# Cross-attention and feed-forward in one kernel: the preparation of the weights in another order

## The reference

```
h = layernorm(x)
q = h @ Wq;  k = context @ Wk;  v = context @ Wv          # 8 heads of 128
x = x + softmax(q k^T / sqrt(128)) v @ Wo + bo
h = layernorm(x)
logits = h @ Wr;  prob = trunc(softmax of the top two logits)
x = x + sq_relu(h @ Ws1) @ Ws2 + sum over experts of prob * (sq_relu(h @ W1) @ W2)
```

## Time and profile before

| | |
|---|---|
| median of 3 runs | 119.76 us (119.48 to 120.51) |
| the profiled execution | 119.6 us, of which the trace spans 117.8 us |
| PE busy | 110.2 us, 94% of the span |
| DVE, ACT, POOL busy | 89.2, 85.0, 62.4 us |
| granted clock of PE, mean | 0.997 of full speed |

### The profile page before, as it was taken

The page is one execution under the profiler, slowest core; times in us unless marked ns, Lnnn a source line. Parts: engine busy times, 40 slices in busy tenths (PEclk is TensorE's granted clock), DMA queues, the critical chain, the costliest instruction groups (busy, mean ns, idle before and its releaser), DMA issues.

```text
span 117.8 us, 3097 instructions
## 1 busy us (share of the span) xinstructions
PE 110.2 (94%) x848; PEld 105.3 (89%) x848; DVE 89.2 (76%) x341; ACT 85.0 (72%) x346; POOL 62.4 (53%) x101
## 2 busy tenths in 40 slices
PE   6999989999899989999999999999999999989950
PEld 6988879998798889999999999999999999978940
DVE  0005999997799697887979797797979778687692
ACT  4025554699559879898998899898978989895200
POOL 2000451479607865786666577757647863429320
PEclk9999999999999999999999999999999999999998
DMA  3999999990000110022004001300400030040033
GB/s 104 341 323 362 347 327 349 351 331 34 0 6 3 49 40 0 6 103 75 0 0 178 0 0 70 108 0 0 178 0 0 37 141 3 3 178 0 26 125 116
DMA packets 11351, 12.70 MB, mean 108 GB/s; under 512 B 976, under 2 KB 9808, under 8 KB 11344
## 3 DMA queue, kind: packets, MB, share of 16 engines
q1 hardware_dynamic: 11344, 12.62, 32.4%
HBM read 8.42 MB, written 2.10 MB: 89 GB/s over the span
## 4 chain that ended last, share of the span: by engine, by line
PE 63%; DVE 20%; DMA 8%; issue 3%; ACT 2%; SPq 2%; DVEq 0%; ACTq 0%
PE o_ps L375 7%; PE o_ps L377 7%; PE o_ps L376 7%; PE s_ps L375 6%; PE s_ps L377 6%; PE s_ps L376 6%; DMA wqt_sb<-in_wq_t 6%; PE g_ps L431 6%; PE f_ps L461 5%; DVE ut_sb L953 3%; DVE row_max L804 2%; PE g_ps L444 2%; DVE wqt_sb L933 2%; PE f_ps L375 2%; DVE wq_mean L929 2%
## 5 line engine op out<-in xcount | busy, mean ns | idle before, releaser
L619 ACT ACTIVATE probs<-s_ps,neg_max,rstd 128x77 f32<-128x77 f32 x128 | 51.5, 425 | 8.2 <-DVE neg_max L812 8.2
L722 POOL TENSOR_TENSOR probs<-probs,recip 128x308 f32<-128x308 f32 x32 | 22.4, 701 | 24.5 <-DVE recip L818 24.3
L619 ACT ACTIVATION_READ_ACCUMULATOR probs<-s_ps,neg_max,rstd 128x1 f32 x128 | 27.3, 214 | 0.0
L375 PE MATMUL o_ps<-u_hi,pt_hi 128*128 128x256 f32 (+1 forms) x80 | 22.7, 284 | 1.1 <-DVE pt_lo L830 0.6
L377 PE MATMUL o_ps<-u_lo,pt_hi 128*128 128x256 f32 (+1 forms) x80 | 22.3, 279 | 0.0
L376 PE MATMUL o_ps<-u_hi,pt_lo 128*128 128x256 f32 (+1 forms) x80 | 22.3, 279 | 0.0
L375 PE MATMUL s_ps<-a_hi,xt_hi 128*128 128x308 f32 x64 | 22.0, 344 | 0.0
L377 PE MATMUL s_ps<-a_lo,xt_hi 128*128 128x308 f32 x64 | 19.5, 304 | 0.0
L376 PE MATMUL s_ps<-a_hi,xt_lo 128*128 128x308 f32 x64 | 19.4, 303 | 0.0
L375 PEld LDWEIGHTS o_ps<-u_hi,pt_hi 128*128 128x128 f32 (+1 forms) x80 | 15.0, 188 | 1.7 <-issue 0.8
L376 PEld LDWEIGHTS o_ps<-u_hi,pt_lo 128*128 128x128 f32 (+1 forms) x80 | 15.1, 188 | 0.0
(11 more groups left out here) (148 smaller groups left out, 249.1 us busy)
## 6 DMA issues: line engine op xcount, KB each, us to landing
xt_sb<-in_x_t SPq DMA_DIRECT2D x8, 256.0 KB, 6.7
x_sb<-in_x SPq DMA_DIRECT2D x8, 256.0 KB, 7.0
x_sb<-x_tr SPq DMA_DIRECT2D x8, 256.0 KB, 2.4
out<-y_sb SPq DMA_DIRECT2D x7, 256.0 KB, 2.3
wqt_sb<-in_wq_t SPq DMA_DIRECT2D x2, 512.0 KB, 7.5
wo_sb<-in_wo SPq DMA_DIRECT2D x1, 1024.0 KB, 9.4
wk_sb<-in_wk_p SPq DMA_DIRECT2D x2, 384.0 KB, 4.3
wv_sb<-in_wv_p SPq DMA_DIRECT2D x2, 384.0 KB, 5.6
```

What stands on the lines that cost most here:

```text
L375: pe.matmul(out_ap, hi, rhs_hi, start=first, stop=False)
L619: e = act.activation(probs[:, par, h * TK:(h + 1) * TK], s_ps[:, 2 * par + half, (h - half * H // 2) * TK:(h - half * H // 2 + 1) * TK], A ...
L722: pool.tensor_tensor(rows, rows, recip[:, par, hs].unsqueeze(2).broadcast_to([P, H // 2, TK]), ALU.mult).then_inc(probs_ready, 1)
```

## The change

The change puts the preparation in another order.

- **Loads.** The context and wk are split into the 128-row part and the tails: ctx main, wk main of heads 0 to 3, wk main of heads 4 to 7, ctx tail, wk tails. wq comes in four quarters of two heads, wv's halves between them: wq 0, wq 1, wv 0, wq 2, wq 3, wv 1. wo goes behind ws1 and wr.
- **PE.** `context_rows` becomes `context_main` and `context_tails`: all eight heads' 128-row matmuls of K, then all the tails. Then A of heads 0 to 3, V main of four heads, A of 4 and 5, V main of the other four, A of 6 and 7, the tails of V. A of heads 4 to 7 goes into `s_ps` again and waits for `a_lo` of the head four before, in place of V's copies. The scores of tile 0 run whole before `wmean`. The scores of tile 2 are cut in halves around the transposes of tile 0, and of tile 3 only a quarter stands ahead of the attention of tile 0.
- **DVE.** wq is centred two heads at a time; `a_lo` of heads 0 and 1 stands ahead of the last quarter. The statistics of tiles 1 and 2 move forward; the last piece of `u_lo` moves ahead of `pt_lo` of tile 0.
- **ACT, POOL.** V's copies move behind `a_hi`; the last `u_hi` ahead of the transposes' copies; ws2's high part and, on POOL, its low part later; the reciprocal roots of tiles 0 to 2 together.

```diff
-        a_banks = [s_ps[:, i, :] for i in range(4)] + once_banks
+        a_banks = [s_ps[:, i, :] for i in range(4)] * 2
...
-            sp.dma_start(ctx_sb[:, :, :], ctx_p).then_inc(ctx_in, 16)
+            def load_wq(i):
+                sp.dma_start(wqt_sb[:, 2 * i:2 * i + 2, :], wq_rows[:, 2 * i:2 * i + 2, :]).then_inc(wq_in[i], 16)
...
+            sp.dma_start(ctx_sb[:, 0, :], ctx_p[:, 0, :]).then_inc(ctx_in, 16)
             for i in range(2):
-                sp.dma_start(wk_sb[:, i, :, :].rearrange("p e c -> p (e c)"), wk_p[:, i, :]).then_inc(wk_in[i], 16)
-            for i in range(2):
-                sp.dma_start(wv_sb[:, i, :, :].rearrange("p e c -> p (e c)"), wv_p[:, i, :]).then_inc(wv_in[i], 16)
-            for i in range(2):
-                sp.dma_start(wqt_sb[:, i * H // 2:(i + 1) * H // 2, :],
-                             wq_t.rearrange("(h p) d -> p h d", p=P)[:, i * H // 2:(i + 1) * H // 2, :]).then_inc(wq_in[i], 16)
+                sp.dma_start(wk_sb[:, i, 0:HG, :].rearrange("p e c -> p (e c)"), wk_p[:, i, 0:HG * P]).then_inc(wk_in[i], 16)
+            sp.dma_start(ctx_sb[:, 1, :], ctx_p[:, 1, :]).then_inc(ctx_tail_in, 16)
+            sp.dma_start(wk_sb[:, :, HG:WB, :].rearrange("p i e c -> p i (e c)"), wk_p[:, :, HG * P:WB * P]).then_inc(wk_tail_in, 16)
+            load_wq(0)
+            load_wq(1)
+            load_wv(0)
+            load_wq(2)
+            load_wq(3)
+            load_wv(1)
...
-                    pe.wait_ge(wq_ready, h // (H // 2) + 1)
-                    if h < 4:
+                    pe.wait_ge(wq_ready, h // 2 + 1)
+                    if h < H // 2:
                         pe.wait_ge(kt_copied, h + 1)
                     else:
-                        pe.wait_ge(vt_copied, h - 3)
+                        pe.wait_ge(alo_ready, h - H // 2 + 1)
...
-                        pe.wait_ge(alo_ready, (half + 1) * H // 2)
+                        pe.wait_ge(alo_ready, (H // 2 + 1, H)[half])
...
-            context_rows(wk_sb, wk_in, [s_ps[:, g, :] for g in range(4)], kt_ready)
-            context_rows(wv_sb, wv_in, once_banks, vt_ready)
-            make_a()
-            scores(0, 0, ((0, 0), (0, 1)))
+            for i in range(2):
+                context_main(wk_sb, i, wk_in[i], s_banks)
+            pe.wait_ge(ctx_tail_in, 16)
+            pe.wait_ge(wk_tail_in, 16)
+            context_tails(wk_sb, s_banks, kt_ready)
+            make_a(range(0, 4))
+            context_main(wv_sb, 0, wv_in[0], once_banks)
+            make_a(range(4, 6))
+            context_main(wv_sb, 1, wv_in[1], once_banks)
+            make_a(range(6, H))
+            context_tails(wv_sb, once_banks, vt_ready)
+            scores(0, 0)
             pe.wait_ge(wsr_in, 32)
-            pe.wait_ge(alo_ready, 7)
+            pe.wait_ge(vt_copied, 3)
...
-            scores(0, 0, ((1, 0), (1, 1)))
             scores(1, 1)
...
-            scores(2, 0)
+            scores(2, 0, ((0, 0), (0, 1)))
             pe.wait_ge(ulo_ready[0], 2)
             transposes_x1(0, 0, transposes(0, 0))
-            scores(3, 1, ((0, 0), (0, 1)))
+            scores(2, 0, ((1, 0), (1, 1)))
+            scores(3, 1, ((0, 0),))
             pe.wait_ge(ulo_ready[1], 1)
             attention(0, 0)
...
+            for i in range(3):
+                centre_wq(i)
+            lo_of_a(0)
+            lo_of_a(1)
+            centre_wq(3)
+            for h in range(2, H):
+                lo_of_a(h)
             dve.wait_ge(x_in[0], 32)
             all_stats_x(0, 0)
+            all_stats_x(1, 1)
+            maxima(0, 0)
+            neg_maxima(0, 0)
             dve.wait_ge(wmean_ready, 1)
...
+            lo_of_u(1, 1)
             dve.wait_ge(x_in[1], 32)
             lo_of_transposes(0, 0)
             lo_of_last(0, 0)
             maxima(2, 0)
             neg_maxima(2, 0)
-            lo_of_u(1, 1)
```

More of the change, by code:

```diff
@@ L177, in program @@
         ws2_in = sem("ws2_in")
-        wq_in = [sem(f"wq_in{i}") for i in range(2)]
+        wq_in = [sem(f"wq_in{i}") for i in range(4)]
         xt_in = [sem(f"xt_in{i}") for i in range(4)]
@@ L343, in _, with context_main, context_tails @@
         def _(pe):
-            def context_rows(w, w_in, banks, ready):
-                for i in range(2):
[L347 to L351, removed]
+            def context_main(w, i, w_in, banks):
+                pe.wait_ge(w_in, 16)
+                for j in range(HG):
+                    h = HG * i + j
+                    pe.matmul(banks[h // 2][:, (h % 2) * BK:(h % 2 + 1) * BK], w[:, i, j, :], ctx_sb[:, 0, :],
+                              start=h % 2 == 0, stop=False)
+            def context_tails(w, banks, ready):
+                for i in range(2):
                     for j in range(2):
@@ L384, in make_ut @@
                         pe.wait_ge(vt_copied, H // 2)
-                    pe.wait_ge(alo_ready, H // 2 + h + 1) if h < H // 2 else pe.wait_ge(ut_copied, h - H // 2 + 1)
+                    if h >= H // 2:
+                        pe.wait_ge(ut_copied, h - H // 2 + 1)
                     if h == 2:
@@ L486, in step @@
                     if isinstance(t, int) and t == 1:
-                        parts = ((1, 0), (1, 1))
+                        parts = ((0, 1), (1, 0), (1, 1))
                     else:
@@ L645, in _ @@
                                ACT.Copy, scale=SCALE2).then_inc(kt_copied, 1)
-            for g in range(H // 2):
-                act.wait_ge(vt_ready, g + 1)
-                act.activation(vt_sb[:, 2 * g:2 * g + 2, :].rearrange("p h n -> p (h n)"), once_banks[g][:, 0:2 * BK],
-                               ACT.Copy).then_inc(vt_copied, 1)
             for h in range(H):
@@ L654, in _ @@
                                ACT.Copy).then_inc(ahi_ready, 1)
-            act.wait_ge(ws2_in, 16)
-            act.activation(ws2_hi[:, :], ws2_sb[:, :], ACT.Copy).then_inc(ws2hi_ready, 1)
+            for g in range(H // 2):
+                act.wait_ge(vt_ready, g + 1)
+                act.activation(vt_sb[:, 2 * g:2 * g + 2, :].rearrange("p h n -> p (h n)"), once_banks[g][:, 0:2 * BK],
+                               ACT.Copy).then_inc(vt_copied, 1)
             exps(0, 0, 0)
@@ L665, in _ @@
                            ACT.Copy).then_inc(ulasthi_ready, 1)
+            hi_of_u(1, 1)
             copy_transposes(0, 0)
-            hi_of_u(1, 1)
+            act.wait_ge(ws2_in, 16)
+            act.activation(ws2_hi[:, :], ws2_sb[:, :], ACT.Copy).then_inc(ws2hi_ready, 1)
             exps(2, 0, 0)
@@ L742, in _ @@
             turned_x(1, 1)
-            rstd_first(0)
-            rstd_first(1)
-            pool.wait_ge(ws2hi_ready, 1)
-            pool.tensor_tensor(ws2_lo[:, :], ws2_sb[:, :], ws2_hi[:, :].bitcast(F32), ALU.subtract).then_inc(ws2lo_ready, 1)
+            for t in range(3):
+                rstd_first(t)
             turned_x(2, 0)
@@ L924, in _, with centre_wq @@
             dve.memset(probs[:, :, HK:KC * P], 0.0).then_inc(fill_ready, 1)
-            for i in range(2):
-                hs = slice(i * H // 2, (i + 1) * H // 2)
+            def centre_wq(i):
+                hs = slice(2 * i, 2 * i + 2)
                 dve.wait_ge(wq_in[i], 16)
@@ L933, in _, with lo_of_a @@
                 dve.tensor_tensor(wqt_sb[:, hs, :], wqt_sb[:, hs, :],
-                                  wq_mean[:, 1, hs].unsqueeze(2).broadcast_to([P, H // 2, D]), ALU.subtract).then_inc(wq_ready, 1)
-            for h in range(H):
+                                  wq_mean[:, 1, hs].unsqueeze(2).broadcast_to([P, 2, D]), ALU.subtract).then_inc(wq_ready, 1)
+            def lo_of_a(h):
                 dve.wait_ge(ahi_ready, h + 1)
```

19 lines of the change are left out of this document (11 added, 8 removed).

## The result

The changed kernel takes 119.2 us (median of 20 runs, 118.84 to 120.34) and the kernel before 120.05 beside it (20 runs, 119.32 to 120.51): ratio 0.995, 95% interval 0.9932 to 0.9968. The change wins 0.5 to 0.85 us; 118.3 was forecast, 0.988 of the 119.76 shown then. The ratios leave out executions over 1.5% slower than the fastest of their kernel: one in e3, two each in e4 and e15, and four of e5's six, which has no ratio for that (e15 with all six would stand at 0.988, not 0.985).

A forecast was written before the change was run, and what follows sets the result against it. The loop was taken as bound by PE from 45 us on, so only time before it could be won: 119.6 us profiled less 1.4 gives 118.2, plus 0.16 for the median, 118.3 forecast; range 117.3 to 119.5.

The forecast's parts named there:

- The transfers of wq: Loads ahead of the preparation: at 346 KB per us wq's first quarter lands at 7.15 us; four more issues delay x by nothing.
- the smaller transfers land later: Rival, chance 0.07: wq's quarters land late, A and first scores pay each us; at 10.1 us the time would be 121.2.
- That rival's point, 8.55 us: Landing of wq's first quarter behind which the changed kernel was to be slower than the kernel before.
- Two signs of being wrong: Among the named signs: a centring that starts after 8 us, and a first score not before 17.9 us.
- the fourth with its delay: DVE's centring of wq's fourth quarter: 1.45 us plus 0.4 more, as it falls beside POOL's split of x.
- K without its waits: PE's preparation: K in one block of each row height takes 3.56 us in place of 3.90.
- PE's waits for DVE at A: In the preparation PE waits some 0.6 us for DVE at three places, leaving 0.6 us won of at most 1.2.
- What is owed: Three matmuls of tile 3's scores, 0.45 us, run behind tile 0's attention and fit in PE's 0.60 us of waits there.
- The split of the gain: Of 1.4 us won at tile 0's attention, 0.6 comes from the preparation and 0.8 from the start behind it.
- The likeliest case: Order runs as forecast, tile 0's attention 1.0 to 1.8 us earlier: 117.9 to 118.7 us, chance 0.56.
- the second one: Rival, chance 0.28: preparation wins nothing, quarters take 1.6 us or land 0.3 late, 119.0; or the owed 0.45 is paid, 118.8.

The follow-up runs named there:

- e3: Changed kernel with the old order from the first scores on, so only the new loads and preparation; 120.18 us, ratio 1.0024 to the kernel before.
- e4: Changed kernel with wk's tails packed into one piece of 2 KB per partition; 119.13 us, ratio 0.9926 to the kernel before.
- e15: e10 run again without further edit; 118.49 us (6 runs), ratio 0.985 to the kernel before.
- e5: Changed kernel with wk's tails and wq's quarters packed to 2 KB per partition; 121.39 us, both profiles at a lower granted clock.
- e1: Changed kernel run again without edit; 119.35 us (12 runs), ratio 0.9956 to the kernel before.
- e6: Changed kernel with context and wk loaded as before the change (three transfers), wq in quarters behind them; 118.49 us, ratio 0.9876 to the kernel before.
- e10: Changed kernel with wk in two transfers again, the context still in two halves; 117.91 us, ratio 0.9822 to the kernel before.
- e12: e6 repeated; 118.34 us, ratio 0.987 to the kernel before.
- e14: e6 with two 4 KB issues of wr put ahead of wq's first quarter; 117.96 us (4 runs), ratio 0.9865 to the kernel before.
- e2: Kernel before with only the changed order from the first scores on, loads and preparation old; 119.31 us, ratio 0.9971 to the kernel before.
- e11: e6 with each half of wk in two transfers of 64 partitions, rows still 3 KB; 118.99 us, ratio 0.9926 to the kernel before.
- e13: Changed kernel with the context's second half and wk's tails issued on ACT's queue; 119.63 us, ratio 0.9974 to the kernel before.

## Why the prediction was wrong

**The step that failed is "The transfers of wq".** It set the first quarter at 6.4 + 256/346 = 7.15 us, taking from two landings of the kernel before that bytes in the queue come at one rate however they are cut, and that the further issues cost nothing. The first quarter came at 8.99, 8.35 and 7.98 us in the three profiles of the split order (the changed kernel, e1, e3), and wk's tails at 8.3 (8.99's execution) where 6.4 was put: both late together, so what is lost is lost before either lands. The rival "the smaller transfers land later" named the mechanism, a late wq that A and the first scores pay for; it looked for the cause in the smaller wq, SP's issues and the number of transfers. Not they but the further transfers of wk lose most of it: with wk in two (e6, e10, e12, e14) and wq still in quarters the first centring is at 6.5 to 7.5 us, on both sides of 7.15. One execution of five with wk in two was late all the same (e15, 8.86), so it is the medians, 117.9 to 118.5 against 119.2 and 119.35, and not one profile, that carry this. That rival's point, 8.55 us, lay between the profiles; its sign (slower) did not come. Two signs of being wrong that the prediction named did: a centring after 8 us, and a first score not before 17.9.

Where the landing was lost can be told closer from the parts. In the changed kernel's profile 14 of the 16 parts were in by 7.17 us, close to the forecast's 7.15 by chance, and the last came at 8.96. The forecast had no term for the wait from most of a transfer to its last part, and none for its spread between executions.

The step had a second fault: its rate of 346 was fitted to landings that trail the bytes moved. Before 7 us e10 had moved 272 x 6 = 1630 KB, where the first quarter is complete after 1178. So bytes of later transfers had moved already, and the two points of the earlier trace rows only carried that lag along. Two slips decide nothing: 346 KB of 1024 bytes per us are 354 GB/s, and 118.2 + 0.16 is 118.36.

**From there on the working held.** Forecast and measured in the changed kernel's profile: first centring to first score 10.15 and 10.40 us; a quarter 1.45 and 1.53 (8.99 to 10.52), the fourth with its delay 1.85 and 1.97 (14.34 to 16.31); first score to first exponential 3.1 and 3.17; to `u_hi` 6.3 and 6.30; to `pt_lo` 3.7 and 3.68; to the attention 0.85 and 0.83. K without its waits: in e10 tails and main parts take 4.85 to 8.35, 3.50 us, 3.56 forecast. PE's waits for DVE at A are there, two of 0.21 and 0.28 us behind the first of 0.92 in the changed kernel's profile, and three of 0.2 to 0.35 in e10's.

**What is owed** cost nothing. The attention of tile 1 follows that of tile 0 by 4.33 us before and by 4.26 after, with three matmuls more between them; only some of this shows as shorter waits (0.43 us between 35 and 45 us where 0.60 were). The rows of tile 1's attention, before and after:

```profile
36.99 0.35 PE L375 MATMUL o_ps<-u_hi,pt_hi 128*128 128x256 f32 x1
```

```profile
37.63 0.37 PE L390 MATMUL o_ps<-u_hi,pt_hi 128*128 128x256 f32 x1
```

Span minus the attention of tile 0 is 118.5 - 33.37 = 85.13 us after and 117.8 - 32.66 = 85.14 before. What is won at the attention is carried to the end whole.

**The split of the gain** into 0.6 us for the preparation and 0.8 for the start held for the start behind the new preparation: span minus the first score fell from 99.91 to 99.11 us. The preparation gave some 0.1 of its 0.6. With wk in two transfers the whole is there (e10 and e15 pooled, all eleven executions, median 118.05, first score by the subtraction above at 17.1). As two gains to be had alone the split was wrong. Alone the start gave 0.35 (e2), since it wants the early `a_lo` of the new preparation, and the preparation nothing (e3), since it wants the transfers.

**The likeliest case** was given 0.56; what came is the second one's time (119.0 or 118.8, within 1%) by another mechanism: its quarters were to be 0.3 us late, and the first was 0.83 to 1.84. That the time still fell inside the stated range, 117.3 to 119.5, is owed to the range's width and not to this step.

Still open: why a third transfer of wk lowers the rate between 4 and 7 us. Piece length (e4, e5, e11) and number of issues and SP's time for them (e14) are excluded, the context as the main cause too (e10); e13 restores the rate in its one profile but not the time, which stays unexplained. The landing also varies within one kernel by as much (7.03 and 8.86 us in e10 and e15). The table says where: 15 of 16 parts were in by 6.79 and 6.76 us there, and the last at 7.01 and 8.84. Why one part trails, no run tells.

## What to carry to other kernels

Where a kernel's start waits on its first transfers, cutting the first large tensor so that a part can be used earlier can make everything behind it later; change the cut alone and time it before the order of the engines is built on it. A landing time interpolated by bytes from a profile holds only for the same cut: give it a range of one to two microseconds here, since one kernel's own executions differ by that much, and read more than one profile. A gain in two parts need not be the sum of what each gives alone, as here, where one of them sets free what the other waits for.
